# LoRA MLP on one core: B factors staged in two buffers, SP and ScalarE queues reordered, one gate product moved ahead of a down product

## What is computed

```python
x = x + conv(x, K) * mask                      # a state-space kernel K per channel, as a causal convolution
x = x + einsum('bct,bcd->bdt', x, W1[cond])    # per-example channel mix
x = x + einsum('bct,bcd->bdt', x, W2[cond])    # again
# MLP with LoRA, rank 16, an adapter per example; H = 512, F = 1376
gate = x @ Wg.T + 0.5 * (x @ Ag[i].T) @ Bg[i].T
up   = x @ Wu.T + 0.5 * (x @ Au[i].T) @ Bu[i].T
act  = silu(gate) * up
x = x + act @ Wd.T + 0.5 * (act @ Ad[i].T) @ Bd[i].T
```

## Time and profile before

| | |
|---|---|
| median of 3 runs | 1175.84 us (1174.17 to 1176.66) |
| the profiled execution, its own time | 1175.31 us |
| its span, first to last instruction | 1173.5 us |
| mean granted TensorE clock | 0.976 of full speed |
| PE busy / PEld busy | 1062.2 us (91%) / 932.3 us (79%) |
| DVE, ACT, POOL busy | 294.4, 441.4, 526.4 us (25%, 38%, 45%) |
| DMA | 135.52 MB, mean 115 GB/s |

### The profile page before, as it was taken

How to read it: one execution, slowest core, us unless ns; L and a number is a source line. 1 busy time by engine, 2 the same in 40 slices (tenths; PEclk the granted TensorE clock), 3 DMA queues, 4 the chain that set the end, 5 groups by cost and what they waited for, 6 DMA issues and landing times.

```text
span 1173.5 us, 19301 instructions
## 1 busy us (share of the span) xinstructions
PE 1062.2 (91%) x6176; PEld 932.3 (79%) x6176; DVE 294.4 (25%) x550; ACT 441.4 (38%) x691; POOL 526.4 (45%) x334
## 2 busy tenths in 40 slices
PE   3577369999999999999999999999999999999998
PEld 3576258888887878888888888787878888888886
DVE  7566212221221222121211222221212221212221
ACT  7543234243333334343424333333433333433331
POOL 0587364343434444443534443444445353544431
PEclk9799679999999999999999999999999999999999
DMA  8688323333324233332333333323333233333321
GB/s 327 221 288 281 121 82 99 102 112 91 108 72 123 69 110 105 98 111 81 109 106 107 89 108 93 114 64 113 93 105 110 81 112 97 107 94 115 96 68 36
DMA packets 100922, 135.52 MB, mean 115 GB/s; under 512 B 26340, under 2 KB 59365, under 8 KB 100901
## 3 DMA queue, kind: packets, MB, share of 16 engines
q1 hardware_dynamic: 99380, 133.35, 37.4%
q10 hardware_dynamic: 1520, 1.92, 0.6%
HBM read 118.21 MB, written 16.99 MB: 115 GB/s over the span
## 4 chain that ended last, share of the span: by engine, by line
SPq 35%; PE 22%; issue 12%; POOL 11%; DMA 11%; ACT 7%; DVE 3%; ACTq 0%; DVEq 0%; POOLq 0%
SPq L339 14%; DMA braw<-in_tb 10%; POOL bst L443 9%; PE ps L979 8%; SPq L188 7%; PE ps L948 6%; ACT bst L572 5%; PE ps L1021 5%; SPq L267 4%; SPq L347 3%; SPq L322 2%; SPq L329 2%; PE ps L969 1%; PE ps L1010 1%; SPq L315 1%
## 5 line engine op out<-in xcount | busy, mean ns | idle before, releaser
L443 POOL TENSOR_TENSOR bst<-braw,bst 128x1024 fp32r<-128x1024 f32 (+1 forms) x96 | 212.2, 2211 | 246.7 <-ACT bst L572 246.7
L979 PE MATMUL ps<-wg_hi,x_hi 128*128 128x512 f32 (+2 forms) x768 | 298.0, 388 | 1.7 <-DVE x_lo L832 1.7
L979 PE MATMUL ps<-wg_hi,x_lo 128*128 128x512 f32 (+2 forms) x768 | 292.1, 380 | 0.0
L979 PE MATMUL ps<-wg_lo,x_hi 128*128 128x512 f32 (+2 forms) x768 | 291.9, 380 | 0.0
L424 POOL TENSOR_TENSOR x_raw<-x_raw,xb 128x512 f32<-128x512 f32 x32 | 41.2, 1286 | 322.2 <-DMA xb<-in_x 322.2
L572 ACT ACTIVATE bst<-braw,odd 128x1024 fp32r<-128x1024 f32 (+1 forms) x96 | 103.6, 1079 | 184.8 <-DMA braw<-in_tb 184.1
L979 PEld LDWEIGHTS ps<-wg_hi,x_lo 128*128 128x128 f32 x768 | 145.2, 189 | 25.7
L979 PEld LDWEIGHTS ps<-wg_hi,x_hi 128*128 128x128 f32 x768 | 145.8, 190 | 22.9 <-issue 2.0
L979 PEld LDWEIGHTS ps<-wg_lo,x_hi 128*128 128x128 f32 x768 | 145.8, 190 | 20.6
L1021 PE MATMUL ps<-wd_hi,at_hi 128*128 128x288 f32 (+1 forms) x704 | 159.0, 307 | 1.8 <-DVE at_lo L855 1.4
L588 ACT ACTIVATE at_hi<-ps 128x512 fp32r<-128x512 f32 (+1 forms) x96 | 54.0, 562 | 274.0 <-PE ps L1010 273.1
(11 more groups left out here) (142 smaller groups left out, 1309.0 us busy)
## 6 DMA issues: line engine op xcount, KB each, us to landing
braw<-in_tb SPq DMA_DIRECT2D x256, 128.0 KB, 2.7
braw<-in_tb SPq DMA_DIRECT2D x128, 96.0 KB, 2.4
adraw<-in_tad SPq DMA_DIRECT2D x128, 88.0 KB, 2.1
ur<-in_xT SPq DMA_DIRECT2D x16, 512.0 KB, 4.3
x1p<-yo SPq DMA_DIRECT2D x16, 512.0 KB, 3.3
x_raw<-x1p SPq DMA_DIRECT2D x32, 256.0 KB, 2.8
xb<-in_x SPq DMA_DIRECT2D x32, 256.0 KB, 3.0
agraw<-in_ta SPq DMA_DIRECT2D x128, 64.0 KB, 2.3
```

Source lines behind the costliest of these rows:

```text
L443: sub(v, b_from(q), v.bitcast(F32), ALU.subtract).then_inc(s["blo"], 1)
L979: last = mm(bank[:, 0:n], x3s[a][:, k, :], wgs[b][:, k, o:o + n], start=(k == 0 and a + b == 0), stop=False, skip_group_check=True)
```

## The change

- `braw` has two buffers, (p+q) mod 2, with a semaphore of landings each (b0, b1). load_b waits for the b_low two parts earlier.
- SP's order per tile becomes: x(t+1), b(t,2), ag, ad, wbd, b(t+1,0), the store of t-1, b(t+1,1), bd. At the very start b(0,1) is loaded between ad and bd.
- ScalarE: silu(t,0), td_high and a_high(0) move ahead of ag_high and x1_high; silu(t,1) ahead of bd_high; ad_high, before ahead of bd_high, moves behind a_high(1) and x3_copy; x3_copy ahead of b_high(t+1,0).
- GpSimd: ad_low goes behind bd_low.
- TensorE: chunk(p,2,0) moves from behind down(t,p,0) to ahead of it.

```diff
@@ -141,7 +141,7 @@
 
 
         mask = sb("mask", [P, GB * RANK])
-        braw = sb("braw", [P, 4 * 2 * P])
+        braw = sb("braw", [P, 2, 4 * 2 * P])
         bst = sb("bst", [P, 2, 4 * 2 * P], F32R)
         bdraw = sb("bdraw", [P, T])
         bdst = sb("bdst", [P, T], F32R)
@@ -164,7 +164,7 @@
             a1 da dch ph tg kuv kps uhi thi usp0 usp1 usp2 usp3 tsp0 tsp1 tsp2 tsp3 whi wlo wlv y0 y1 y2 y3
             ev0 ev1 ev2 ev3 yst0 yst1 done wz msk
             xin xsum x1hi x1lo wbd x3mm x3n x3t x3hi x3lo
-            ag aghi aglo ad adhi adlo b bhi blo bd bdhi bdlo
+            ag aghi aglo ad adhi adlo b0 b1 bhi blo bd bdhi bdlo
             bfree la tm tmt thi2 tlo2 gu silu mul att ahi alo td tdm tdt tdhi tdlo accd evac ost""".split() + [
             f"wl{n}" for n in range(NW)]
         s = {n: sem("s_" + n) for n in names}
@@ -230,9 +230,9 @@
             n = PAIRS[q][1] - PAIRS[q][0]
             return bst[:, (p + q) % 2, 0:n * 2 * P].rearrange("p (u j f) -> p j u f", u=2, f=P)
 
-        def b_from(q):
+        def b_from(p, q):
             n = PAIRS[q][1] - PAIRS[q][0]
-            return braw[:, 0:n * 2 * P].rearrange("p (j u f) -> p j u f", u=2, f=P)
+            return braw[:, (p + q) % 2, 0:n * 2 * P].rearrange("p (j u f) -> p j u f", u=2, f=P)
 
         block = ctx.enter_context(nc.Block())
 
@@ -329,15 +329,15 @@
                     sp.dma_start(adraw[:, b * WAD:(b + 1) * WAD], tad[e[b]].rearrange("a p w -> (a p) w")
                                  ).then_inc(s["ad"], 16)
 
-            def load_b(t, e, q, first=False):
-                if not first:
-                    sp.wait_ge(s["blo"], t * 3 + q)
+            def load_b(t, e, p, q, free=None):
+                if free is not None:
+                    sp.wait_ge(s["blo"], free)
                     sp.sem_inc(s["bfree"], 1)
                 o, w = PAIRS[q][0] * 2 * P, (PAIRS[q][1] - PAIRS[q][0]) * 2 * P
                 for b in range(GB):
                     rows = tb[e[b], :, o:o + w].rearrange("a k w -> (a k) w")
-                    sp.dma_start(braw[b * 2 * RANK:(b + 1) * 2 * RANK, 0:w],
-                                 rows.unsqueeze(1).to_broadcast([RANK, 2, w])).then_inc(s["b"], 16)
+                    sp.dma_start(braw[b * 2 * RANK:(b + 1) * 2 * RANK, (p + q) % 2, 0:w],
+                                 rows.unsqueeze(1).to_broadcast([RANK, 2, w])).then_inc(s[f"b{(p + q) % 2}"], 16)
 
             def load_bd(t, e, first=False):
                 if not first:
@@ -353,18 +353,18 @@
                 sp.dma_start(out[bass.ds(row, TN), :], outb[:]).then_inc(s["ost"], 16)
 
             def tile_io(t, p, here, there, mixes, first=False, last=False):
-                load_b(t, here, 1)
                 if not last:
                     load_x(t + 1)
+                load_b(t, here, p, 2, t * 3 + 1)
+                if not last:
                     load_ag(t + 1, there)
                     load_ad(t + 1, there)
                     load_wbd(t if not first else None, mixes, 1 - p)
-                load_b(t, here, 2)
-                if not last:
-                    load_b(t + 1, there, 0)
+                    load_b(t + 1, there, 1 - p, 0, t * 3 + 2)
                 if not first:
                     store_out(t - 1)
                 if not last:
+                    load_b(t + 1, there, 1 - p, 1, t * 3 + 3)
                     load_bd(t + 1, there)
 
             def block_io(i, first=False, last=False):
@@ -375,8 +375,9 @@
                 if first:
                     load_x(0, True)
                     load_ag(0, here[0:GB], True)
-                    load_b(0, here[0:GB], 0, True)
+                    load_b(0, here[0:GB], 0, 0)
                     load_ad(0, here[0:GB], True)
+                    load_b(0, here[0:GB], 0, 1)
                     load_bd(0, here[0:GB], True)
                 tile_io(i * 2, 0, here[0:GB], here[GB:], mixes, first=first)
                 tile_io(i * 2 + 1, 1, here[GB:], there, after, last=last)
@@ -440,7 +441,7 @@
             def b_low(t, p, q):
                 pool.wait_ge(s["bhi"], t * 3 + q + 1)
                 v = b_view(p, q)
-                sub(v, b_from(q), v.bitcast(F32), ALU.subtract).then_inc(s["blo"], 1)
+                sub(v, b_from(p, q), v.bitcast(F32), ALU.subtract).then_inc(s["blo"], 1)
 
             def bd_low(t):
                 pool.wait_ge(s["bdhi"], t + 1)
@@ -462,10 +463,9 @@
                     ag_low(t + 1)
                     x1_low(t + 1)
                 b_low(t, p, 2)
+                bd_low(t)
                 if not last:
                     ad_low(t + 1, 1 - p)
-                bd_low(t)
-                if not last:
                     b_low(t + 1, 1 - p, 0)
 
             with pool.Fori(0, NBLK - 1) as i:
@@ -566,10 +566,11 @@
                 copy(ad_view(wd_hi, p), ad_from(), ACT.Copy).then_inc(s["adhi"], 1)
 
             def b_high(t, p, q, free=None):
-                act.wait_ge(s["b"], (t * 3 + q + 1) * 16 * GB)
+                slot = (p + q) % 2
+                act.wait_ge(s[f"b{slot}"], (t * 3 + q - slot) * 8 * GB + 16 * GB)
                 if free is not None:
                     act.wait_ge(s["gu"], free)
-                copy(b_view(p, q), b_from(q), ACT.Copy, scale=odd[:, 0:1]).then_inc(s["bhi"], 1)
+                copy(b_view(p, q), b_from(p, q), ACT.Copy, scale=odd[:, 0:1]).then_inc(s["bhi"], 1)
 
             def bd_high(t, first=False):
                 act.wait_ge(s["bd"], (t + 1) * 16 * GB)
@@ -609,22 +610,21 @@
                     a_high(t - 1, 2)
                 t_high(t)
                 b_high(t, p, 1, None if first else t * 3)
+                silu(t, p, 0)
+                if not first:
+                    td_high(t - 1)
+                a_high(t, 0)
                 if not last:
                     ag_high(t + 1)
                     x1_high(t + 1)
-                silu(t, p, 0)
-                if not first:
-                    td_high(t - 1)
-                a_high(t, 0)
                 b_high(t, p, 2, t * 3 + 1)
-                if not last:
-                    ad_high(t + 1, 1 - p, None if first else t)
+                silu(t, p, 1)
                 bd_high(t, first)
-                silu(t, p, 1)
                 a_high(t, 1)
                 if not last:
+                    x3_copy(t + 1, 1 - p)
+                    ad_high(t + 1, 1 - p, None if first else t)
                     b_high(t + 1, 1 - p, 0, t * 3 + 2)
-                    x3_copy(t + 1, 1 - p)
                     x3_high(t + 1)
 
             tile_act(0, 0, first=True)
@@ -1059,6 +1059,7 @@
                 if not first:
                     lora_b_down(t - 1, 1 - p)
                 lora_b(t, p, 1)
+                chunk(p, 2, 0)
                 if not first:
                     pe.wait_ge(s["evac"], t)
                 else:
@@ -1066,7 +1067,6 @@
                     pe.wait_ge(s["wlv"], 3)
                 pe.wait_ge(s["adlo"], t + 1)
                 down(t, p, 0)
-                chunk(p, 2, 0)
                 a_turn(t, 1)
                 if not last:
                     mix(t + 1, 1 - p)
```

More of the change, by code:

```diff
@@ L611, in tile_act @@
                 b_high(t, p, 1, None if first else t * 3)
-                if not last:
-                    ag_high(t + 1)
-                    x1_high(t + 1)
                 silu(t, p, 0)
@@ L618, in tile_act @@
                 a_high(t, 0)
+                if not last:
+                    ag_high(t + 1)
+                    x1_high(t + 1)
                 b_high(t, p, 2, t * 3 + 1)
-                if not last:
-                    ad_high(t + 1, 1 - p, None if first else t)
+                silu(t, p, 1)
                 bd_high(t, first)
-                silu(t, p, 1)
                 a_high(t, 1)
                 if not last:
+                    x3_copy(t + 1, 1 - p)
+                    ad_high(t + 1, 1 - p, None if first else t)
                     b_high(t + 1, 1 - p, 0, t * 3 + 2)
-                    x3_copy(t + 1, 1 - p)
                     x3_high(t + 1)
```

## The result

The changed kernel takes 1115.92 us, median of 4 runs (1114.27 to 1116.23); the kernel before, in the same comparison, 1175.26 us (4 runs). The ratio is 0.9486, 95% interval 0.9466 to 0.9505. The forecast was 1117, the range 1113 to 1131. The profiled execution of after took 1114.27 us, with a span of 1112.4 us against 1173.5: 61.1 us less. Two executions of the kernel before, in the comparison of e9 and e10, fell in a slow state (1778 and 5909 us) and are left out of the ratios.

What follows compares the result with a forecast made beforehand. The prediction took odd tiles as bound by TensorE's own work and even tiles as waiting on ScalarE's queue. Terms 39.2 + 8.4 + 10.3 = 57.9 us, from 1175.3, gave 1117 us, range 1113 to 1131.

Steps and rivals of the forecast that it cites:

- tile 0: First tile: with its own buffer b(0,1) comes early, ending a_turn(0,0)'s 7.95 us wait and slow clock after it; 10.3 us.
- stalls of even tiles: TensorE's waits in even tiles, 2.80 us per pair over 14 pairs, expected to go: 39.2 us.
- TensorE's exchange: chunk(t,2,0) ahead of down(t,0) on TensorE covers a pause of about 0.27 us in 31 tiles: 8.4 us.
- the ring: Not in the prediction: closed chain of B loads, b_high, b_low, bdraw, entries in the kernel before, one turn 63.13 us.
- all three releasers: silu(t,0), silu(t,1) and x3_copy in ScalarE's queue, said to stall even tiles by standing behind work waiting for DMAs.
- these three: The SP order with second braw, ScalarE order and GpSimd order together, credited with 39.2 us.
- 1.25, 0.46 and 0.85: Even-tile lags in us at a_turn(t,0), a_turn(t,1) and x3_turn, each expected to go by a move in ScalarE's list.
- 1, a stall that stays: Even tiles: a ScalarE wait remains or comes anew, costing 0.46 to 1.25 us a pair; 1124 to 1136 us; chance 0.14.
- 2, the exchange gives nothing: TensorE's pause at down(t,0) comes from changing operands, so moving chunk gains nothing; 1125 us; chance 0.12.
- 3, slower: SP's odd-tile list ends late, so late x holds b_low(t,1) and lora_b(t,1); 1194 us if 10 us late; chance 0.02.
- 4, the buffer doesn't matter: SP's own issue time binds, so the second braw gains nothing; 1172 to 1178 us; chance 0.02.
- 5, the clock: Even tiles' 42 short stalls also lower TensorE's clock; removing them gives 97 us more, near 1020 us; chance 0.01.

Runs made afterwards that it cites:

- e9: Kernel before, one braw, with only SP's load_bd(t) moved between b(t,2) and b(t+1,0): 1136.12 us, ratio 0.9685 to before.
- e10: Kernel before with load_bd(t) moved between b(t,2) and b(t+1,0), and chunk(p,2,0) ahead of down(t,p,0): 1134.22 us, ratio 0.9667 to before.
- e2: Kernel after with TensorE's order undone, chunk(p,2,0) back behind down(t,p,0): 1125.16 us, ratio 0.9581 to before.
- e1: Kernel before with only TensorE's new order, chunk(p,2,0) ahead of down(t,p,0): 1173.97 us, ratio 1.0006 to before.
- e3: Kernel before with only ScalarE's and GpSimd's new orders, still one braw: 1169.96 us, ratio 0.9963 to before.
- e6: Kernel after with ScalarE's and GpSimd's orders undone: 1125.64 us, ratio 0.959 to before.
- e5: Kernel before with only the second braw buffer and its semaphores, all orders as before: 1137.43 us, ratio 0.9697 to before.
- e4: Kernel after with SP's old order, two buffers kept: 1116.74 us, ratio 0.951 to before.
- e7: Kernel after with the second braw buffer undone, new orders kept: 1380.11 us, ratio 1.1756 to before.
- e8: Kernel after with 12 small extra loads on SP at the start of each even tile, ahead of load_x: 1135.42 us, ratio 0.9676 to before.

## Why the prediction was right, and where it wasn't

**The sum.** 57.9 us were forecast; the medians differ by 59.3, the spans by 61.1. By terms:

| term | forecast | tiles 2 to 29 and tile 0, measured | what the runs say |
|---|---|---|---|
| stalls of even tiles | 39.2 | 14 x (63.30 - 60.46) = 39.8, by e2 | right in size, the mechanism wrong |
| TensorE's exchange | 8.4 | 28 x 0.27 = 7.6; whole kernel 9.2 by the medians of e2 and after | right, but only with the ring open |
| tile 0 | 10.3 | 10.4 | right |
| tile 30 | 0 | 0.75 | left out |
| up to the first t_turn | 0 | 2.2 | varies between executions |

**The step that failed** is the first one, "an odd tile is bound by TensorE's own work, and an even tile waits", with its reason, "all three releasers run in ScalarE's queue, behind work that waits for DMAs". Both are true of the rows and don't say what sets the time. TensorE was busy throughout the odd tile because the ring's slack happened to be spent in the even one. e1 shows it: 0.3 us a tile taken from TensorE came back as waiting. e3 shows that ScalarE's order wasn't the cause either. The prediction did name SP's late start and the single braw, but as the cause of late copies, and never as a chain with a length of its own. The size of the term came out right since 63.30 - 60.50 is the excess of the pair over TensorE's work by any reading: for the kernel before that was luck. For the kernel after it was not, since the walk through the queues there showed every load in time, and nothing was left to wait for.

**The credit** was given to "these three" together, which was prudent; the prediction's text on ScalarE then assigned 1.25, 0.46 and 0.85 to three moves in its list. e3 and e6 refute this split. In steady state the buffer alone gives 2.32 of the 2.80 us of a pair (e5). Either SP's new order or ScalarE's and GpSimd's gives the rest (e4, e6), and neither is needed beside the other. The parts don't add: on before they measure 0, 4, and 36 us, together 40; taken from after singly, 9, 10, 1 and 264.

**Positions.** In GpSimd's list b_low(t,2) was to end at 14.6 and bd_low at 15.9; they end at 14.62 and 15.87 (582.99 + 1.28 less 568.40). silu(t,1) was to start at 11.5 and x3_copy at 18.2; they start at 11.63 and 17.87. The walk through the queues of after was sound (one slip: it puts load_x at -1.6 by the old tile of 30.25; by the forecast's own 29.98 it is -1.3, against -1.58 measured). The same walk was never closed into a turn for before; had it been, it would have given 63.1.

**Tile 0.** a_turn(0,0) waits no longer, and the clock stands at 1.00 where the earlier trace rows had 0.53. e6 adds a condition that the prediction didn't have: "a_turn(0,0) waits for silu(0,0) alone" needs the new order of ScalarE (or GpSimd; e6 undoes both) too, since with the old one the wait is 7.0 us. This is where the orders of ScalarE and GpSimd earn their 9.7 us.

**The rivals.** 1, a stall that stays: none did; e5 shows how it looks, 0.5 a pair. 2, the exchange gives nothing: no, by e2, but yes in e1 and e10. 3, slower: the path and the free 5 us are confirmed by e8, and after is that far from it. 4, the buffer doesn't matter: the reverse; without it the other edits cost 207 us over before (e7). 5, the clock: even tiles stood at 1.00 before and after, with the stalls of the earlier trace rows, up to 1.09 us, in between, and at 1.00 also behind the longest stall of an even tile, 1.82 us in tile 4, so nothing was to be had there. The Trainium skill, "TensorE: Matmul & The Clock Gate", section "A second HAM failure mode: psum-queue depth-cycling", has short idle times between groups of matmuls lower the clock again and again; the stalls of before didn't, and the slightly longer ones of e3 did at times (below).

**Left open.** How far the 104 us of e7 are clock. The largest waits of TensorE in after, one of 17.2 us for x_lo before the first MLP tile and 12.8 for kk, lie outside this change, and no run touched them.

## What to carry to other kernels

Read the chain that ended last before the tiles and stalls: TensorE was busy 91% of the time here and had 22% of the chain; it wasn't the bound, and the edit to it was worth nothing until the ring was opened. When a loop's period is longer than the work of its busiest engine, follow one resource (here one staging buffer) round until it comes back to the same instruction, and add up that turn; the time that an issue queue spends inside it counts, even for loads that nobody waits for (e9). Price an edit by the bound that holds once the other edits are in, and expect the parts of a change not to add.

## What the hardware showed that I had not expected

- **Clock after short waits.** In tiles 2 to 29 of the kernel before the granted clock stayed at 1.00, with single waits of TensorE of up to 1.82 us. In e3 a_turn(t,1) waits in each of the 14 even tiles. Behind the twelve waits of 1.06 to 1.80 us the granted clock of the next 5 us was 1.00, the 2.4 GHz level; behind the two of 1.90 and 2.43 us it was 0.66, near the 1.2 GHz level for most of the stretch, and those two tiles took 34.6 and 34.9 us instead of 32.8. Tile 14 of e3, before and behind its 1.90 us wait:

```profile
610.00:616.00 6.00, 4.11 (x23) 3.29 (x21) 0.69 (x1) 2.24 (x3) 1.32 (x2) 1.00 0.25 79
616.00:621.00 5.00, 4.98 (x17) 4.03 (x18) 0.69 (x1) 2.58 (x3) 3.58 (x3) 0.66 0.20 59
```

The ring took up part of that loss: the next even tile was shorter each time (31.49 and 32.27).

- **Price of an issue.** On SP's queue a small load of the same source took 0.49 us (5.90 us for 12, e8), a wbd load about 0.78 and a braw load 0.75. So the price isn't one for all loads; what in a load sets it, no run here separates.
